# Graph convolution kernel: the normalised rows written by ScalarE as x·rstd + bias, with a bias made by GpSimd

## The reference, cut to what matters

```python
def _layernorm(x, axis=-1, eps=1e-5):
    m = jnp.mean(x, axis=axis, keepdims=True)
    v = jnp.var(x, axis=axis, keepdims=True)
    return (x - m) / jnp.sqrt(v + eps)
...
    h = jnp.maximum(_layernorm(x, axis=-1), 0.0)
    x = x + _L0_gnn_ref(h, adj, L0_gnn_w_se, ...)
    h = jnp.maximum(_layernorm(x, axis=-1), 0.0)
    x = x + _L1_gnn_ref(h, adj, L1_gnn_weight, L1_gnn_bias)
    return x
```

## Time and profile before

| | us |
|---|---|
| median of 3 runs | 2045.76 (2044.67 to 2048.74) |
| the profiled execution, its own time | 2044.45 |
| its span, first to last instruction | 2042.6 |
| PE busy | 1902.4 (93%) |
| DVE busy | 1483.0 (73%) |
| ACT busy | 797.3 (39%) |
| POOL busy | 378.3 (19%) |

### The profile page before, as it was taken

One profiled execution on the slowest core, in us unless ns is written; L12 is line 12 of the kernel. 1 busy time (PEld: TensorE's weight loads), 2 busy tenths in 40 slices (PEclk: granted clock), 3 DMA queues, 4 the chain that ended last, 5 costly groups with the idle time before them and its releaser, 6 DMA issues.

```text
span 2042.6 us, 37528 instructions
## 1 busy us (share of the span) xinstructions
PE 1902.4 (93%) x13018; PEld 1434.6 (70%) x13018; DVE 1483.0 (73%) x3288; ACT 797.3 (39%) x1478; POOL 378.3 (19%) x555
## 2 busy tenths in 40 slices
PE   2877989999975999999999999999999999999997
PEld 2566767764434777777777777787777777877775
DVE  3887878852234777877777778777777787777775
ACT  3864545544224333333333333333333333333332
POOL 1021111100012222221221222212212222122120
PEclk9999989999987999999999999999999999999998
DMA  2086565556234222322222223222222232222220
GB/s 99 12 295 231 193 217 193 198 215 249 98 140 146 71 82 68 97 74 74 96 68 87 83 68 99 71 74 96 68 92 79 68 100 70 76 94 68 91 79 16
DMA packets 162857, 224.40 MB, mean 110 GB/s; under 512 B 15863, under 2 KB 112878, under 8 KB 162030
## 3 DMA queue, kind: packets, MB, share of 16 engines
q1 hardware_dynamic: 162798, 223.62, 32.8%
HBM read 133.39 MB, written 90.18 MB: 109 GB/s over the span
## 4 chain that ended last, share of the span: by engine, by line
PE 63%; DVE 3%; ACT 2%; issue 0%; DMA 0%; POOL 0%; ACTq 0%; POOLq 0%; DVEq 0%
PE ps_rz L1241 26%; PE ps_n L1241 13%; PE ps_l L1241 13%; PE ps_b L1241 9%; DVE nmp L1347 2%; ACT nmp L1342 2%; PE ps_adj L1267 1%; PE ps_d L1250 1%; DMA rows<-spectra 0%; ACTq L1163 0%; PE ps_s L1201 0%; DVE sum_rz L1387 0%; POOL conv_x L1218 0%; POOL conv_v L1223 0%; PE ps_d L1465 0%
## 5 line engine op out<-in xcount | busy, mean ns | idle before, releaser
L1396 ACT ACTIVATE tanh_rz<-sum_rz,w_scale 128x512 f32<-128x512 f32 x128 | 92.5, 722 | 472.7 <-DVE sum_rz L1387 472.7
L832 PE MATMUL m_ps<-big 128*128 128x512 f16 (+1 forms) x1152 | 268.6, 376 | 5.1 <-DVE ysb L742 3.2
L1241 PE MATMUL ps_rz<-w_ih,nmp 128*128 128x512 f32 x768 | 206.1, 403 | 11.6 <-DVE nmp L1347 11.4
L1421 POOL TENSOR_TENSOR x_new<-xin,new 128x256 f32<-128x256 f32 x128 | 93.7, 732 | 662.6 <-ACT new L1414 662.6
L1241 PE MATMUL ps_rz<-w_ih,conv_t 128*128 128x512 f32 x768 | 209.3, 407 | 0.1
L832 PEld LDWEIGHTS m_ps<-big 128*128 128x128 f16 x1152 | 112.4, 98 | 109.7 <-DVE ysb L742 4.7
L1241 PE MATMUL ps_rz<-w_hh,ht 128*128 128x512 f16 x768 | 186.6, 379 | 0.9 <-DVE sum_n L1390 0.9
L1241 PE MATMUL ps_l<-w_l,h2t 128*128 128x512 f16 x768 | 179.1, 383 | 1.4 <-DVE h2t L1477 1.4
L1241 PEld LDWEIGHTS ps_rz<-w_ih,nmp 128*128 128x128 f32 x768 | 134.7, 188 | 50.6 <-DVE nmp L1347 26.7
L742 DVE SCALAR_TENSOR_TENSOR ysb<-m_ps,ysb 128x512 f16<-128x512 f32 x96 | 66.0, 689 | 119.8 <-ACT ysb L668 119.6
L1241 PEld LDWEIGHTS ps_rz<-w_ih,conv_t 128*128 128x128 f32 x768 | 134.8, 189 | 24.3 <-DVE conv_t L1233 0.3
(11 more groups left out here) (211 smaller groups left out, 3796.3 us busy)
## 6 DMA issues: line engine op xcount, KB each, us to landing
xin<-in_x SPq DMA_DIRECT2D x128, 256.0 KB, 2.9
spectra<-ysb SPq DMA_DIRECT2D x96, 256.0 KB, 2.0
rows<-spectra SPq DMA_DIRECT2D x64, 384.0 KB, 3.5
x_normed<-xhat SPq DMA_DIRECT2D x64, 256.0 KB, 3.4
h_turned<-ht SPq DMA_DIRECT2D x64, 256.0 KB, 2.5
adj_in<-in_adj SPq DMA_DIRECT2D x64, 256.0 KB, 3.7
ht<-h_turned SPq DMA_DIRECT2D x64, 256.0 KB, 3.3
xhat<-x_normed SPq DMA_DIRECT2D x64, 256.0 KB, 2.9
```

The lines of the kernel that those rows point to most:

```text
L832: last = pe.matmul(dest, x_, w_, start=n == 0, stop=n == 11, skip_group_check=True)
L1241: last = pe.matmul(dest, stationary(dl), moving(wl), start=start and n == 0, stop=stop and n == 2, **kw)
L1396: act.activation(tanh_rz[:, i, :], sum_rz[:, i, :], ACT.Tanh, scale=w["scale"][:, 4:5]).then_inc(S["rz_tanh"], 1)
L1421: pool.tensor_tensor(x_new[:, i, :], xin[:, p, i, :], new[:, i, :], ALU.add).then_inc(S["x_new_done"], 1)
```

## The change

`normalise` leaves VectorE. ScalarE writes the same tile as `Identity(x * rstd + shift)` with both operands per partition, so the subtraction of the mean becomes an added bias, shift = -mean * rstd. GpSimd makes that bias: after the addition of eps it multiplies the mean by -1, then does the power as before, then one more multiplication; `rstd_done` is now signalled by that last one. On ScalarE the step stands in slot q after `split_h(q)` and a `split_y`, before `split_h1(q-1)`. It also waits for the load of x. Two new small buffers and two semaphores are added, and `layer_rstd` waits until the tile two graphs back has been written. Nothing changes in the loops of TensorE and SyncE, nor outside `convolution`.

```diff
                 def layer_rstd(f):
                     pool.wait_ge(stats_done, f + 1)
+                    if f >= 2:
+                        pool.wait_ge(xhat_done, f - 1)
                     pool.tensor_tensor(rstd[:, f % 2, :], meanvar[:, f % 2, :, 1], eps[:, :], ALU.add).then_inc(var_done, 1)
+                    pool.tensor_scalar(minus_mean[:, f % 2, :], meanvar[:, f % 2, :, 0], -1.0, 1.0, ALU.mult,
+                                       ALU.mult).then_inc(mean_done, 1)
                     pool.wait_ge(var_done, f + 1)
                     pool.tensor_tensor(rstd[:, f % 2, :], rstd[:, f % 2, :], minus_half[:, :],
-                                       ALU.pow).then_inc(rstd_done, 1)
+                                       ALU.pow).then_inc(power_done, 1)
+                    pool.wait_ge(mean_done, f + 1)
+                    pool.wait_ge(power_done, f + 1)
+                    pool.tensor_tensor(shift[:, f % 2, :], minus_mean[:, f % 2, :], rstd[:, f % 2, :],
+                                       ALU.mult).then_inc(rstd_done, 1)
...
             def _(act):
+                def normalise(f):
+                    act.wait_ge(rstd_done, f + 1)
+                    act.wait_ge(x_loaded[f % 2], 16 * (f // 2 + 1))
+                    if f >= 2:
+                        act.wait_ge(turned, f - 1)
+                        act.wait_ge(xhat_stored[f % 2], 16 * (f // 2))
+                    for t in range(H):
+                        last = act.activation(xhat[:, f % 2, t, :], xin[:, f % 2, t, :], ACT.Identity,
+                                              scale=rstd[:, f % 2, t:t + 1], bias=shift[:, f % 2, t:t + 1])
+                    last.then_inc(xhat_done, 1)
...
                 act.wait_ge(cleared, 3)
+                normalise(0)
                 for q in range(SLOTS):
                     if q < graphs:
                         split_h(q)
                     if unit_at(q, 0) is not None:
                         split_y(unit_at(q, 0))
+                    if q + 1 < graphs:
+                        normalise(q + 1)
                     if 0 <= q - 1 < graphs:
                         split_h1(q - 1)
...
-                def normalise(f):
-                    dve.wait_ge(rstd_done, f + 1)
-                    if f >= 2:
-                        dve.wait_ge(turned, f - 1)
-                        dve.wait_ge(xhat_stored[f % 2], 16 * (f // 2))
-                    for t in range(H):
-                        last = dve.tensor_scalar(xhat[:, f % 2, t, :], xin[:, f % 2, t, :], meanvar[:, f % 2, t, 0:1],
-                                                 rstd[:, f % 2, t:t + 1], ALU.subtract, ALU.mult)
-                    last.then_inc(xhat_done, 1)
...
                 layer_stats(0)
-                normalise(0)
                 for q in range(SLOTS):
...
-                    if q + 1 < graphs:
-                        normalise(q + 1)
```

More of the change, by code:

```diff
@@ L433, in convolution @@
         rstd = sb("rstd", [P, 2, H])
+        minus_mean = sb("minus_mean", [P, 2, H])
+        shift = sb("shift", [P, 2, H])
         minus_half = sb("minus_half", [P, H])
@@ L450, in convolution @@
         var_done = sem("var_done")
+        mean_done = sem("mean_done")
+        power_done = sem("power_done")
         rstd_done = sem("rstd_done")
```

## The result

The changed kernel takes 2101.43 us (median of 4 runs, 2099.83 to 2103.99) beside 2046.27 for the kernel before (the three executions further up and one more), a ratio of 1.0268 with a 95% interval of 1.0256 to 1.0281. It is slower, and inside the predicted range; the forecast of 2110 was 9 us too high. The profiled execution has a span of 2097.9 us where the one before had 2042.6: 55.3 us more.

The account below looks back on a forecast made before the run. It took a VectorE-GpSimd loop to bound slots without main chunks and TensorE those with them. 16 x 1.45 + 0.8 + 44 x 0.96 - 1.0 = 65.2 us on 2044.45 gave 2110, range 2093 to 2130.

Parts of the forecast that it names:

- the ring: Loop of statistics, GpSimd, normalise and split_h1 on ScalarE, VectorE's splits, next statistics: 5.80 us a slot for 4.35; chance 0.76.
- GpSimd, 1.52 (1.42 to 1.61): Loop piece on GpSimd, from the eps addition to the hand-over to ScalarE: 1.52 us where it was 1.00.
- ScalarE, 0.95 (0.82 to 1.05): Loop piece on ScalarE, from the start of the new activation pair to split_h1: 0.95 us.
- The hop to VectorE 0.63, the rest 1.60: ScalarE's split_h1 start to VectorE's, a new piece of 0.63 us; from there to the next statistics 1.60 as before.
- Units' splits, 0.32 on average: In slots with main chunks, a unit's split on VectorE lies in the loop in two of four: 6.12 us a slot.
- The long waits for x, -1: VectorE's two waits for loads behind a large store: longer slots hide more, TensorE at half clock gives part back, -1 us.
- First slots +0.8: In the first two slots normalise now stands behind ScalarE's split_h, adding 0.8 us.
- What would show it: Signs: VectorE waiting about 2 us a slot, ScalarE over 1, L628 to activation 1.5, TensorE below 90% busy in 294 to 423.
- (a): Rival: VectorE's relief decides and the kernel gets faster, -18 us in slots without main chunks, to 2026; chance 0.04.
- (c): Rival: GpSimd's small operations cost as much as its power, 0.7 us each, +1 us in 60 slots, 2170; chance 0.03.
- (d): Rival: slots overlap better than the loop drawn, 5.57 us a slot, -14 us over 60 slots, 2096; chance 0.07.
- (b): Rival: TensorE's clock falls to 1.2 GHz in slots without main chunks, +11 us, 2121; chance 0.07.

Follow-up runs that it names:

- e5: The changed kernel without GpSimd's two new operations, the activation taking the mean itself as its bias; 2078.71 us, ratio 1.0163.
- e1: The changed kernel with ScalarE's normalise(q+1) placed behind split_h1(q-1) instead of ahead of it; 2061.84 us, ratio 1.0089.
- e2: The changed kernel with VectorE's statistics made one graph earlier, the activation left where the change put it; 2052.62 us, ratio 1.0039.
- e6: The kernel before with the same pair of activations added on ScalarE, on unread tiles of ones, without waiting for GpSimd; 2048.53 us, ratio 1.0020.
- e4: The kernel before with GpSimd's new operations alone, VectorE still normalising but waiting for the last of them; 2052.87 us, ratio 1.0036.

## Why the prediction was right, point by point

- **What bounds, and the ring.** Right. The ring was drawn from the order of the loops and priced from rows of before, and came out at 5.80 for 5.71. e5 shortens one link by 0.39 and the slot by 0.38; e1 takes one out (5.71 to 4.93, where I had expected 5.10); e2 cuts the ring, and both pauses go. e6 and e4 add the work without the links and move it little.
- **Statistics to GpSimd, 0.78 + 0.32.** Measured 0.78 + 0.33.
- **GpSimd, 1.52 (1.42 to 1.61).** Mis-sized: 1.38, below my lower end. I took the pace of a chain in which each operation waits for the last, 0.27 to 0.30 from start to start; without a wait the next starts 154.05 - 153.89 = 0.16 and 154.20 - 154.05 = 0.15 later. 0.14 in 60 slots is 8 us, most of the miss. Behind the power it was a little longer than I had it: 155.04 - 154.20 = 0.84, for 0.78 to 0.81.
- **ScalarE, 0.95 (0.82 to 1.05).** Measured 1.00; one activation 0.589. The row of PSUM inputs was the right neighbour, the one with a scale alone was too cheap. The 0.05 that I was short here hides 3 us of GpSimd's 8, which is luck. As an estimate, the Trainium skill's formula (ScalarE: Activation LUTs, "What ACT_TABLE_LOAD costs") gives 585 ns for one and 0.98 us from the pair's start to the next instruction; the trace agrees, with 589 ns and 1.00 us.
- **The hop to VectorE 0.63, the rest 1.60.** Measured 0.61 and 1.61. The path over ScalarE's `split_x`, which I had put within 0.05 of this one, was some 0.4 shorter and so not in the ring: its end comes 156.75 + 0.85 - 156.27 = 1.33 after the start of `split_h1`, where before it was 1.71. That didn't touch the sum.
- **Units' splits, 0.32 on average.** Measured (6.30 - 5.71) / 2 = 0.30; slots of 6.00 for 6.12.
- **The long waits for x, -1.** Mis-sized: -4.4. The 44 slots take 273.64, of which 44 x 6.00 = 264.0, so 9.6 us over for 14.0 before. The fixed time after the large store held for the first wait and not for the second. From SyncE's issue of the store to the statistics that waited it is 192.08 - 181.97 = 10.11 us before and 214.31 - 204.19 = 10.12 after, but then 282.51 - 269.58 = 12.93 before and 315.13 - 304.13 = 11.00 after; why the second came sooner isn't shown. The two long slots take 10.23 and 10.51 us for 10.21 and 12.16, which over ordinary slots of 6.00 and 5.16 is 8.7 for 12.1. What I gave back for TensorE at half clock wasn't there: the following slots took 5.71 and 6.30, their usual lengths.
- **`negate` and `split_h` hidden.** Right: the slot with `negate` shown above is 5.71 and the mean of all sixteen, with and without it, 5.70.
- **First slots +0.8.** Measured +0.5.
- **The sum.** 65.2 forecast, 55.3 measured in the span. Of the 9.9 that it came out lower, 6 are GpSimd less ScalarE's pair, with the hop (0.10 in 60 slots), 1 the splits (0.02 in 44 slots), 3.4 the long waits and 0.3 the first slots; the ends, which I had at nothing, took 0.7 more.
- **What would show it.** VectorE waits 2.49 a slot (about 2), ScalarE 1.94 (over 1), L634 to the activation 1.38 (1.5). TensorE in 294 to 423, the window that I had named, is busy 112.81 of 129.00 us, 87%, but one of the long waits lies in it. Without a long wait it is 70.39 of 78.30, just under 90%, and 117.32 of 129.00 in 330 to 459, 91%: no longer full, as the ring needs, but at the edge of the sign that I gave. The turn waits for ScalarE as said.
- **The rivals.** (a), faster by the relief of VectorE, needed GpSimd's result to be there in time; VectorE was relieved and spent it waiting. (c) falls with 0.19 an operation, (d) with 5.71, which is nearer to the forecast than to its 5.57. Half of (d) was so, GpSimd at its lower end, and the total, 2101.4, is nearer to its 2096 than to 2110; but the long waits gave 3.4 of that, which (d) didn't have. (b) is half true, below.

## What to carry to other kernels

Before moving a step to a less busy engine, write down what stands behind it there and follow the ring until it closes: add the start-to-start times of its links, and a link across engines for each hand-over. A busy share says nothing of such a ring; ScalarE had 26 us free in 70 and the step still cost 1.35 us a slot. If the ring is what binds, cut it first (here the statistics one graph earlier and one more input buffer), and only then ask which engine should have the step; here, with both, the two choices came within 0.5 us of each other.

## What the runs showed of the hardware that I had not expected

TensorE's granted clock fell to half, 1.2 GHz, in the middle of the first stage, where TensorE's longest wait for ScalarE is 1.4 us, and it cost nothing. Busy time by stretch of the changed kernel, columns as in the earlier trace rows:

```profile
148.00:152.00 4.00, 1.98 (x17) 1.43 (x15) 1.51 (x6) 2.43 (x6) 1.20 (x4) 1.00 0.49 188
152.00:156.00 4.00, 3.92 (x22) 2.92 (x23) 2.35 (x7) 2.06 (x4) 1.21 (x4) 0.58 0.88 320
156.00:160.00 4.00, 3.29 (x32) 2.77 (x30) 3.09 (x9) 3.03 (x6) 0.41 (x3) 1.00 0.53 192
```

After a stretch with TensorE busy 1.98 of 4.00 us the clock is 0.58 in the next (part of it at half), then at full, 2.4 GHz, again; over the 16 slots it is 0.92. In the slot from 152.78 `conv1` ran at half clock: its six matmuls take 1.50 us where they take 0.83 in the next.

```profile
153.76 1.50 PE L804 MATMUL c_ps<-w1t,ht 128*128 128x259 f16 x6
...
157.90 0.83 PE L804 MATMUL c_ps<-w1t,ht 128*128 128x259 f16 x6
```

This slot took 158.49 - 152.78 = 5.71 us like the rest: `conv1` has until ScalarE's `split_h1`, and that waits for GpSimd anyway. The trace has four such dips in the 16 slots, and every one of these slots takes 5.70; why the clock fell in these and not in others of the same pattern isn't shown. My rival (b) had the clock falling as it did, but held for good, and charged 11 us for it.

The second surprise is GpSimd's pace: small operations on 128x2 that don't wait for one another follow at 0.15 to 0.16 us, less than the 0.19 that one lasts.
